# Cross-attention scores as three fp32r products, a second bank for key products, and all attention-transpose copies on ScalarE

## What is computed

```python
x = x + cross_attention(layernorm(x), ctx, ctx)   # 16 heads of 32, 2048 keys
x = x + self_attention(layernorm(x))              # 16 heads, own norm inside
x = x + ffn(layernorm(x))                         # router takes 1 of 4 experts, 512 -> 2048 -> 512
# cross attention:
q, k, v = Q @ Wq + bq, K @ Wk + bk, V @ Wv + bv
scores  = einsum('bhqd,bhkd->bhqk', q, k) / sqrt(32)
out     = softmax(scores) @ v @ Wo + bo
```

## Time and profile before

| | |
|---|---|
| median of 3 runs | 547.36 us (545.71 to 547.57) |
| the profiled execution | 545.29 us, of it span 543.2 us |
| PE busy | 519.1 us, 96% of the span |
| DVE, ACT, POOL busy | 294.8, 210.0, 38.3 us |
| mean granted PE clock | 0.989 |
| chain that ended last | PE 92%, DVE 2%, issue 2%, ACT 2%, DMA 2% |

### The profile page before, as it was taken

One profiled execution on the slowest core, in us unless ns is written; L12 is line 12 of the kernel. 1 busy time (PEld: TensorE's weight loads), 2 busy tenths in 40 slices (PEclk: granted clock), 3 DMA queues, 4 the chain that ended last, 5 costly groups with the idle time before them and its releaser, 6 DMA issues.

```text
span 543.2 us, 8865 instructions
## 1 busy us (share of the span) xinstructions
PE 519.1 (96%) x3582; PEld 371.0 (68%) x3582; DVE 294.8 (54%) x606; ACT 210.0 (39%) x305; POOL 38.3 (7%) x32
## 2 busy tenths in 40 slices
PE   7999999999998999999999999978999999999995
PEld 6777777677776777988776677636485445877652
DVE  4635525657676652453596685542355635976332
ACT  4110007273735431456025355255046206755220
POOL 0220000000395000000000000000000010000000
PEclk8999999999998999999999999989999999999999
DMA  8800000000450002330100000780796876775000
GB/s 277 324 0 1 1 1 0 1 2 3 162 212 14 2 2 77 100 135 0 59 2 1 1 2 1 276 344 1 278 402 233 326 285 231 268 290 225 1 19 19
DMA packets 11310, 62.21 MB, mean 115 GB/s; under 512 B 1540, under 2 KB 2564, under 8 KB 4484
## 3 DMA queue, kind: packets, MB, share of 16 engines
q1 hardware_dynamic: 11272, 61.66, 30.1%
HBM read 61.13 MB, written 0.52 MB: 113 GB/s over the span
## 4 chain that ended last, share of the span: by engine, by line
PE 92%; DVE 2%; issue 2%; ACT 2%; DMA 2%; SPq 0%; POOLq 0%; DVEq 0%; ACTq 0%
PE ps L965 41%; PE ps L1028 11%; PE ps L1217 10%; PE ps L1014 6%; PE ps L1043 6%; PE ps L1264 5%; PE ps L1244 3%; PE ps L1245 3%; PE ps L1246 3%; DMA wv_raw<-in_xWv 2%; PE ps L959 1%; PE ps L1227 1%; DVE Pm L610 1%; PE ps L1141 1%; DVE Kr L590 1%
## 5 line engine op out<-in xcount | busy, mean ns | idle before, releaser
L376 ACT COPY PT<-ps 128x512 f32<-128x512 f32 x96 | 53.3, 588 | 108.0 <-PE ps L1028 108.0
L1028 PEld LDWEIGHTS ps<-ident,Pm 128*128 128x128 f32 x512 | 56.7, 141 | 21.8 <-issue 18.3
L1028 PE MATMUL ps<-ident,Pm 128*128 128x128 f32 x512 | 69.3, 277 | 1.6 <-ACT PT L376 0.7
L610 DVE TENSOR_SCALAR_CACHE_REDUCE Pm<-ps,small 128x512 f32<-128x512 f32 x96 | 66.4, 748 | 7.3 <-PE ps L1014 7.1
L368 ACT ACTIVATE Pm<-Pm,small 128x2048 f32<-128x2048 f32 x32 | 64.2, 2009 | 14.2 <-DVE Pm L610 14.2
L1217 PE MATMUL ps<-w1raw,z 128*128 128x512 f32 x128 | 59.0, 610 | 3.3 <-DVE z L793 3.3
L965 PE MATMUL ps<-ctxH,wkH 128*128 128x512 f32 x124 | 51.9, 418 | 2.4 <-DVE Kr L590 2.1
L965 PE MATMUL ps<-wvH,ctxH 128*128 128x512 f32 x128 | 51.4, 402 | 0.8 <-DVE wvL L654 0.8
L965 PE MATMUL ps<-wvH,ctxL 128*128 128x512 f32 x128 | 49.9, 390 | 0.0
L965 PE MATMUL ps<-wvL,ctxH 128*128 128x512 f32 x128 | 49.9, 390 | 0.0
L965 PE MATMUL ps<-ctxL,wkH 128*128 128x512 f32 x124 | 49.3, 398 | 0.0
(11 more groups left out here) (164 smaller groups left out, 717.2 us busy)
## 6 DMA issues: line engine op xcount, KB each, us to landing
w1raw<-in_W SPq DMA_DIRECT2D x16, 1024.0 KB, 7.7
w2raw<-in_W SPq DMA_DIRECT2D x16, 1024.0 KB, 4.8
raw<-in_ctxT SPq DMA_DIRECT2D x7, 1024.0 KB, 4.9
woF<-in_ffn_Wo SPq DMA_DIRECT2D x4, 1024.0 KB, 14.4
raw<-in_ctxT SPq DMA_DIRECT2D x2, 512.0 KB, 5.4
wv_raw<-in_xWv SPq DMA_DIRECT2D x2, 512.0 KB, 7.8
wq<-in_xWq SPq DMA_DIRECT2D x1, 1024.0 KB, 12.3
wS<-in_xWo SPq DMA_DIRECT2D x1, 1024.0 KB, 6.9
```

The source lines that it names most:

```text
L376: act.copy(PT[:, c % 2, i, :, :].rearrange("p k t -> p (k t)"), ps[:, T_BANKS[i % 2], :]).then_inc(pt_act, 1)
L610: dve.tensor_scalar(Pm[:, i, c * CH:(c + 1) * CH], ps[:, i, :], -1.0, mx[:, p % 2, i, c - 1:c] if c else NOT_YET, ALU.mult, ALU.min, accum ...
L1028: last = pe.transpose(ps[:, T_BANKS[i % 2], j * P:(j + 1) * P], Pm[:, i, c * CH + j * P:c * CH + (j + 1) * P], ident[:])
```

## The change

Five parts. **Scores.** ACT writes a rounded fp32r part of queries and keys (`qH`, `KrH`), DVE the remainder (`qL`, `KrL`), and a block's scores are three rounds of four fp32r products: high x high, query remainder x high, high x key remainder. `Kr` with four blocks becomes rings of three. **Banks.** The product of keys 1 goes to bank 3, the score bank of head 3, and no longer waits for keys 0 to be drained; keys 2 waits for keys 0 alone. **Copies.** All four heads' `PT` copies are on ACT, with one semaphore. **Buffers.** `wS` moves from a place of its own to PT's, so its first load waits for the weighted values of batch 0; `wo` gets two buffers and is loaded twice. **Order.** Behind pass 4 the self attention stands one value product later; the addition of `xbo` to x moves to pass 0, and half the shuffles of `outputs2_T(0)` move to ACT.

```diff
-        Kr = at("Kr", [P, C, CH], F32, 176)
+        KR = 3
+        KrH = at("KrH", [P, KR, CH], F32R, 176)
+        KrL = at("KrL", [P, KR, CH], F32R, 182)
+        qH = at("qH", [P, G, TOK], F32R, 188)
+        qL = at("qL", [P, G, TOK], F32R, 196)
-        wS = at("wS", [P, KT, D], F32, 184)
+        wS = at("wS", [P, KT, D], F32, 160)
+        wo2 = [at(f"wo2_{b}", [P, KT, D], F32, kb) for b, kb in enumerate((24, 48))]
-        K_BANK, PV_BANK = 6, 7
+        K_BANK, K2_BANK, PV_BANK = 6, 3, 7
...
# SP
-            sp.wait_ge(x_added, B)
+            sp.wait_ge(pv_mm, C * G)
             sp.dma_start(wS[:], a["xWo"]).then_inc(wS_in, 16)
...
+                if n == 7:
+                    sp.wait_ge(qkv_mm[1], 2)
+                    sp.dma_start(wo2[1][:], a["wo"]).then_inc(wo2_in[1], 16)
...
# ACT
+            def keys(p, c):
+
+                n = p * C + c
+                bank = K2_BANK if p and c == 1 else K_BANK
+                act.wait_ge(k_mm, n + 1)
+                if n >= KR:
+                    act.wait_ge(s_mm, (n if c == C - 1 else p * C) * HPG - (2 * HPG if c == C - 1 else 0))
+                act.activation(KrH[:, c % KR, :], ps[:, bank, :], ACT.Identity, bias=bias3[:, 1, p % G:p % G + 1],
+                               scale=1.0).then_inc(k_hi, 1)
...
                 act.activation(qT[:, m, :], ps[:, (m + 2) % 4, 0:TOK], ACT.Identity, bias=bqs[:, m:m + 1],
                                scale=SCALE).then_inc(q_done, 1)
+                act.activation(qH[:, m, :], ps[:, (m + 2) % 4, 0:TOK], ACT.Identity, bias=bqs[:, m:m + 1],
+                               scale=SCALE).then_inc(q_done, 1)
...
                     exponentials(p - 1, 0)
+                if p < NP:
+                    keys(p, 0)
+                if p != G + 1:
                     exponentials(p - 1, 1)
                     if late:
                         reciprocals_T(p - 2)
                     exponentials(p - 1, 2)
+                if p < NP:
+                    keys(p, 1)
                 probs_T(p - 1, 0, 0)
                 probs_T(p - 1, 0, 1)
                 if p != G + 1:
                     exponentials(p - 1, 3)
+                if p < NP:
+                    keys(p, 2)
                 probs_T(p - 1, 0, 2)
+                probs_T(p - 1, 0, 3)
...
# DVE
-                dve.wait_ge(k_mm, n + 1)
-                if p:
-                    dve.wait_ge(s_mm, (n - C + 1) * HPG)
-                dve.tensor_scalar(Kr[:, c, :], ps[:, K_BANK, :], bias3[:, 1, p % G:p % G + 1], None,
-                                  ALU.add).then_inc(k_done, 1)
+                bank = K2_BANK if p and c == 1 else K_BANK
+                dve.wait_ge(k_hi, n + 1)
+                dve.scalar_tensor_tensor(KrL[:, c % KR, :], ps[:, bank, :], bias3[:, 1, p % G:p % G + 1],
+                                         KrH[:, c % KR, :].bitcast(F32), ALU.add, ALU.subtract).then_inc(k_done, 1)
...
+            for m in range(G):
+                dve.wait_ge(q_done, 2 * (m + 1))
+                dve.tensor_tensor(qL[:, m, :], qT[:, m, :], qH[:, m, :].bitcast(F32), ALU.subtract).then_inc(q_split, 1)
...
# PE, keys
-                if p * C + c:
-                    pe.wait_ge(k_done, p * C + c)
+                if p * C + c and not (p and c == 1):
+                    pe.wait_ge(k_done, p * C + c - (1 if p and c == 2 else 0))
...
+                if p and c == 1:
+                    pe.wait_ge(s_done, p * C * HPG)
+                product(ps[:, K2_BANK if p and c == 1 else K_BANK, :], [(w[:, k, f], t[:, k, :]) for k in range(KT)
...
# PE, scores
-                for i in range(HPG):
-                    q = slice(DH * i, DH * (i + 1))
-                    if n:
-                        pe.wait_ge(s_done, (n - 1) * HPG + i + 1)
-                    pe.matmul(ps[:, i, :], qT[q, g, b * T:(b + 1) * T], Kr[q, c, :], start=True, stop=True)\
-                        .then_inc(s_mm, 1)
+                if p and c == 0:
+                    pe.wait_ge(k_done, n + 2)
+                terms = ((qH, KrH), (qL, KrH), (qH, KrL))
+                for k, (l, r) in enumerate(terms):
+                    for i in range(HPG):
+                        q = slice(DH * i, DH * (i + 1))
+                        if n and k == 0:
+                            pe.wait_ge(s_done, (n - 1) * HPG + i + 1)
+                        last = pe.matmul(ps[:, i, :], l[q, g, b * T:(b + 1) * T], r[q, c % KR, :], start=(k == 0),
+                                         stop=(k == len(terms) - 1))
+                        if k == len(terms) - 1:
+                            last.then_inc(s_mm, 1)
```

More of the change, by code:

```diff
@@ L258, in _ @@
             sp.dma_start(wS[:], a["wq"]).then_inc(wS_in, 16)
[L259 removed]
+            for k, w in enumerate(("wk", "wv")):
                 sp.wait_ge(qkv_mm[0], k + 1)
@@ L384, in reciprocals_T @@
                 act.copy(RT[:], ps[:, PV_BANK, P:2 * P]).then_inc(r_copied, 1)
+            act.wait_ge(bias_in, 16)
+            keys(0, 0)
             for j in (0, 2):
@@ L438, in values2, with outputs2_T @@
                 act.copy(V2[b][:].rearrange("p g d -> p (g d)"), ps[:, 4 * b, :]).then_inc(v2_ready, 1)
+            def outputs2_T(b):
+                act.wait_ge(cN_ready, b + 1)
+                for i in range(2, HPG):
+                    for a in range(HPG):
+                        act.copy(cT[b][DH * a:DH * (a + 1), :, :]
+                                 .rearrange("p m (g i t) -> p m g i t", i=HPG, t=TPH)[:, :, :, i, :],
+                                 cN[b][DH * i:DH * (i + 1), :, :].rearrange("p g (t c) -> p g t c", t=TPH)[:, :, :, a::HPG]
+                                 .rearrange("p g t m -> p m g t")).then_inc(cT_act[b], 1)
             def masks(b):
@@ L472, in _ @@
                     exponentials(p - 1, 3)
+                if p < NP:
+                    keys(p, 2)
                 probs_T(p - 1, 0, 2)
+                probs_T(p - 1, 0, 3)
                 for c in range(1, C):
-                    if p == G + 3 and c == 3:
-                        masks(0)
-                    for i in range(3):
+                    for i in range(HPG):
+                        if p == G + 3 and c == 3 and i == 0:
+                            masks(0)
+                        if c == 2 and i == 0 and p < NP:
+                            keys(p, 3)
                         probs_T(p - 1, c, i)
+                    if p == G + 1 and c == 1:
+                        outputs2_T(0)
                 if p == G:
@@ L524, in _ @@
             act.copy(b1H[:], b1raw[:]).then_inc(b1_hi, 1)
[L525 to L531, removed]
+            outputs2_T(1)
             transposed(yT[1], x2T_mm, 1, XT_BANKS[1], x2T_done)
@@ L673, in _ @@
                     values(0, c, j)
+                if c == 1:
+                    dve.wait_ge(xbo_in, 16)
+                    dve.wait_ge(norm_done, B)
+                    for b in range(B):
+                        dve.tensor_tensor(x[:, b, :], x[:, b, :], xbo[:], ALU.add).then_inc(x_added, 1)
+                    dve.wait_ge(x_added, B)
                 negative_scores(0, c)
@@ L1020, in probs_T @@
                 n = p * C + c
[L1021 to L1026, removed]
+                if HPG * n + i >= 2:
+                    pe.wait_ge(pt_done, HPG * n + i - 1)
                 for j in range(JT):
@@ L1168, in attention2_out @@
             def attention2_out(b):
-                pe.wait_ge(wS_in, 16 * 5)
-                pe.wait_ge(cT_dve[b], HPG * (2 if b else HPG))
-                if b:
-                    pe.wait_ge(cT_act[b], 2 * HPG)
-                else:
+                pe.wait_ge(wo2_in[b], 16)
+                pe.wait_ge(cT_dve[b], 2 * HPG)
+                pe.wait_ge(cT_act[b], 2 * HPG)
+                if not b:
                     pe.wait_ge(s_done, (G + 2) * C * HPG)
-                product(ps[:, O2_BANKS[b], :], [(cT[b][:, k, :], wS[:, k, :]) for k in range(KT)]).then_inc(o2_mm, 1)
+                product(ps[:, O2_BANKS[b], :], [(cT[b][:, k, :], wo2[b][:, k, :]) for k in range(KT)]).then_inc(o2_mm, 1)
             def normalized_T(b):
```

75 lines of the change are left out of this document (30 added, 45 removed).

## The result

The changed kernel takes 542.4 us (median of 4 runs, 540.0 to 542.8), before 547.47 us beside it; ratio 0.9895, 95% interval 0.9847 to 0.9943. That is 5.1 us less, where 4.3 us were forecast; the interval allows 3.1 to 8.4 us. The profiled execution of the changed kernel took 542.14 us, 3.15 us less than the one before, where 541.0 was forecast for it; its span is 540.4 us. One of the ten executions of e2, the profiled one, was in a slower state of the chip, so e2's time is the median of the other nine, and of its profile only distances and waits inside the passes are read.

A forecast was written before the change was run, and what follows sets the result against it. The prediction took PE, busy 96% of the span, as the bound. Its terms summed to -4.3 us, 545.29 to 541.0 us for the profiled execution, so 543.0 us for the median; range 539.5 to 549 us.

The forecast's parts named there:

- The scores: Score blocks on PE: three fp32r rounds take 0.90 us, not 1.07; 0.17 us saved in each of 32 blocks, -5.4 us.
- The first rival: Score rounds on PE expose their weight loads: 1.26 us a block, 553.1 us in all; chance 0.11.
- The second rival: Narrow score rounds gain nothing, each paying the entry: 1.10 us a block, 548.6 us in all; chance 0.14.
- the fourth: Rival: the four heads' fp32r score products don't run beside each other, 1.90 us more per block, about 602 to 606 us; chance 0.03.
- Queries and masks: Scores 0 wait for the split queries, +0.8 us once; masks of pass 7 wait for both key copies, +0.65 us.
- The stall of pass 4: Start of pass 4: the reciprocals' matmul waits longer for DVE's copy `rexp` by what pass 3 gains, +0.7 us.
- The 2.2 us that I named as its sign: Sign to look for at the start of pass 4: a reciprocals' wait of 2.2 us.
- The head on ACT: Start of a pass: ACT's key copies delay the last exponential to 11.5 us; PE waits about 0.1 us in pass 2.
- the wait which I said would change its name: Pass 1: the wait of keys 1 goes, but the late last exponential delays scores 0, +0.3 us.
- the 0 to 0.3 us that I gave as a sign: Passes 1 and 2: PE's wait on an exponential before the transposes of head 3, 0 to 0.3 us.
- The third rival: ACT becomes the bound at the head of a pass, its copies costing 0.6 us more: 544.2 to 545.4 us; chance 0.13.
- The second bank: Waits around keys 1: -0.9 us in pass 5, +0.3 in pass 1, -0.5 in pass 4.

The follow-up runs named there:

- e2: The changed kernel without the second bank: keys 1 back in bank 6 and the three old waits back; 549.9 us, ratio 1.0053.
- e10: The changed kernel with two score rounds in place of three, the product with the key remainder left out; 538.7 us in one run.
- e11: The changed kernel with each of the three score rounds made twice, six in all; 563.8 us in one run.
- e6: The changed kernel with four pieces of PE's order moved (masks, keys, weighted values, and pass 4's reciprocals' matmul behind keys 1); 534.2 us, ratio 0.978.
- e5: The changed kernel with DVE, not ACT, writing the high part of keys 0 and 1 in passes 1 to 7; 542.06 us, ratio 0.9916.
- e9: The changed kernel with head 3's PT copies back on DVE; 542.0 us, ratio 0.9895.
- e1: The kernel before with the second bank for keys 1 alone, nothing else of the change; 541.4 us, ratio 0.9895.
- e3: The changed kernel with a block's twelve score products ordered head by head; 540.9 us in one run.
- e4: The changed kernel with scores as one plain fp32 product per head, the copies and subtractions still made; 545.65 us, ratio 0.9973.
- e7: The changed kernel with the edits of both e5 and e6; 532.7 us, ratio 0.9738.
- e12: e7 with DVE writing the high part of keys 0 and 1 in passes 1 to 3 only, ACT in 4 to 7; 531.55 us, ratio 0.9716.

## Why the prediction was right, point by point

The sum held term by term in the passes: at scores 3 of pass 7 the changed kernel is 3.7 us ahead in the profiles, where the terms up to there make 4.1, and it is 0.5 us late already 14 us in, where PE waits for the splits of what was loaded first. The medians differ by 5.1 and the profiled executions by 3.15, on either side of 4.3; that the two are 2 us apart is within what executions of one kernel differ by, and neither can judge a term.

**The scores.** 0.90 us a slot and 0.17 us less: as forecast, and e10 and e11 show the two numbers behind it. The first rival fell: the loads of the second round run beside the first (rows above), and six rounds cost 1.59 us, not 2.1. On this the Trainium skill's rule that I weighed (TensorE: Matmul & The Clock Gate, Part 3, The mechanism) does not describe this kernel; the same section also lets a load go ahead when it is for the background weight buffer, and with that the loads here would agree. The second rival (entry in each round) and the fourth fell with the same rows: the second and third round follow at 0.24 us, and four products start together.

**Queries and masks.** The wait for the query remainders is 1.4 us where 0.6 was (+0.8 forecast), the wait before the masks 1.7 where 0.94 was (+0.65 forecast).

**The stall of pass 4.** It is there with 2.5 us, 0.7 us more than before: the term of the sum. (The 2.2 us that I named as its sign do not follow from my own 1.8 + 0.7.) DVE's copy again ends with POOL's instruction, at 170.32 and 170.23, and keys 1 follow 0.25 us behind. With the matmul behind keys 1 (e6) the stall is gone. The clock is another matter: it fell behind the stall before, in the changed kernel, e2, e5, e9 and e10, and did not in e1 and e3, with a wait of 2.3 us there, nor in e4 and e11. My sum left it out, and it did not change between the two profiles.

**The head on ACT.** Pass 1: scores 0 started 0.24 us later relative to the pass's start at unchanged slots (+0.3 forecast), with a wait of 1.25 us on the exponential. That is the wait which I said would change its name; the 0 to 0.3 us that I gave as a sign held in pass 2 only (0.20 us). e5 confirms the cause. Pass 2 lost 0.11 us (+0.1 forecast), and so did pass 3, where I had nothing. The third rival needed copies that take 0.6 us more; they did not (key copies at 0.58 us from one start to the next, two `PT` copies in 1.07).

**The second bank.** Its terms came true where I put them: 0.95 us in pass 5 (-0.9) and 0.5 us in pass 4. What I did not see are two parts that cancel. In each of passes 2 and 3 the bank takes away 0.3 us which only the distance between starts shows (e1), and ACT's key copies put back 0.4 us (e5 against the changed kernel). I had the copies at 0.1 and 0, and the bank at 0. That these errors have opposite signs is luck. And the bank's worth was asked against the kernel before only: there it is 3.2 us in heads and bodies, besides the clock, but in the changed kernel its absence costs 7.3 us (e2), where I expected 2.6.

**Copies, buffers and order.** Nothing, as forecast (e9 for the copies). For the loads of `xWo` and `wo` no wait of PE is in the trace; they weren't tried by themselves.

So the parts do not add up. The bank alone brings 5.4 us (e1). Everything else of the change without it costs 2.9 us (e2, 0.5% slower than before), although its slots save 5.4. Both together bring 5.1. Only when ACT's key copies and four pieces of PE's order were moved did the kernel come to 13 to 16 us below before (e7, e12).

**Left open:** how much of a median difference of 1 to 2 us is the clock. One fall of the clock costs about 1.6 us in the profiles, and executions of one kernel differ with the mean granted clock (of e4: 543.6 at 0.995, 547.2 at 0.984). Why the clock falls near the end of some executions with PE busy, and why only some stalls of pass 4 bring it down, was not settled.

## What to carry to other kernels

Price a released wait by the distance between starts on the waiting engine, not by the list of waits; a wait shorter than the modelled tail of a matmul is not listed. Before work is put on an engine that is 39% busy, write out its queue in the stretch where it is late (here four exponentials of 2 us): of two key copies, 1.2 us, ahead of the last exponential, 0.65 us fitted into the slack, and 0.4 us went to PE in each of passes 2 and 3. And a second buffer is to be judged together with the latency of who drains it: in heads and bodies it was worth 3.2 us with one engine draining and 7.3 us with two.

## What the runs showed of the hardware

Twelve products, four heads of 32 rows by three terms, take 0.90 us issued in rounds and 0.92 us issued head by head (e3), and start in the same rounds: a product whose rows are free starts ahead of one that stands before it in the program. A weight load of 0.18 us for rows in use hides behind a product of 0.23 us. In 9 of the 14 profiles the clock fell to its lower level 2 to 3 us behind the start of the last expert bias products (4 rows), in the changed kernel between 508 and 514 us, with PE fully busy; in the other five, the kernel before and e9 among them, the same products ran at full clock.
